# A decay mix with a routed low-rank layer on one Trainium2 core: a partial sum in the third group, the second group's routing one scan later, weight chunks in another order

## What is computed

```python
ek, ekv = exp(min(f, 30)), exp(min(f, 30)) * f
nf, df = scan(a = a*decay + ekv), scan(b = b*decay + ek)       # forward in time
nb, db = the same two, backward in time
euk  = exp(min(u + f, 30))
y    = sigmoid(x) * (nf + nb - ekv + euk*f) / max(df + db - ek + euk, 1e-8) * gain
h      = silu(y @ rw1.T + rb1)                                  # 64 wide
logits = (h @ rw2.T + rb2)[:, :16] + gates
coeff  = softmax over the two largest logits, 0 elsewhere       # 16 experts
base   = y @ W.T + bias                                         # 1024 x 1024
delta  = ((y @ A.T) * coeff) @ B                                # 16 experts of rank 16
out    = x + base + delta
```

## Time and profile before

| | us |
|---|---|
| median of 3 runs | 656.72 |
| lowest and highest | 656.48, 657.44 |
| the profiled execution, its own time | 657.03 |
| its span in the trace (first to last instruction) | 654.9 |
| TensorE busy | 586.5 |
| VectorE busy | 506.1 |
| GpSimd busy | 374.6 |
| ScalarE busy | 372.1 |

### The profile page before, as it was taken

The page is one execution under the profiler, slowest core; times in us unless marked ns, Lnnn a source line. Parts: engine busy times, 40 slices in busy tenths (PEclk is TensorE's granted clock), DMA queues, the critical chain, the costliest instruction groups (busy, mean ns, idle before and its releaser), DMA issues.

```text
span 654.9 us, 6960 instructions
## 1 busy us (share of the span) xinstructions
PE 586.5 (90%) x2562; PEld 472.7 (72%) x2562; DVE 506.1 (77%) x562; ACT 372.1 (57%) x446; POOL 374.6 (57%) x190
## 2 busy tenths in 40 slices
PE   0145899989989979999999989999999999999997
PEld 0134686768867857888788867888788878888786
DVE  7999999999989999998999989997899121032202
ACT  6788899979759775648565775486355310020100
POOL 1799999999949955765566657575357201000100
PEclk9977899999989989999999999999999999999999
DMA  6335566576716821786142722354132303050112
GB/s 201 119 103 181 175 209 181 159 163 130 149 56 126 198 94 38 178 219 208 49 145 72 249 65 78 116 175 146 49 113 87 122 0 97 0 161 1 49 48 81
DMA packets 32097, 78.45 MB, mean 120 GB/s; under 512 B 4608, under 2 KB 4800, under 8 KB 32064
## 3 DMA queue, kind: packets, MB, share of 16 engines
q1 hardware_dynamic: 28608, 69.62, 33.1%
q0 software_dynamic: 3456, 8.39, 7.9%
HBM read 57.03 MB, written 25.17 MB: 126 GB/s over the span
## 4 chain that ended last, share of the span: by engine, by line
PE 47%; DVE 26%; POOL 11%; issue 6%; ACT 6%; DMA 4%; SPq 0%; POOLq 0%; DVEq 0%; ACTq 0%
PE acc L1071 15%; PE acc L1073 14%; PE acc L1072 14%; DVE mix L866 4%; DVE mix L861 4%; DVE mix L857 4%; DVE mix L888 3%; DMA yr<-x_cm 2%; POOL mix L727 2%; POOL y_lo L737 2%; DVE eu L876 2%; DVE yr L895 2%; POOL mix L702 2%; POOL yr L708 2%; DVE kv L871 1%
## 5 line engine op out<-in xcount | busy, mean ns | idle before, releaser
L1071 PE MATMUL acc<-y_hi,wa_hi 128*128 128x512 f32 x638 | 254.9, 400 | 51.0 <-POOL y_lo L737 46.2
L1072 PE MATMUL acc<-y_lo,wa_hi 128*128 128x512 f32 x638 | 251.3, 394 | 0.0
L1073 PE MATMUL acc<-y_hi,wa_lo 128*128 128x512 f32 x638 | 251.2, 394 | 0.0
L1071 PEld LDWEIGHTS acc<-y_hi,wa_hi 128*128 128x128 f32 x638 | 121.8, 191 | 80.8 <-POOL y_lo L737 48.0
L1073 PEld LDWEIGHTS acc<-y_hi,wa_lo 128*128 128x128 f32 x638 | 121.5, 190 | 26.0
L1072 PEld LDWEIGHTS acc<-y_lo,wa_hi 128*128 128x128 f32 x638 | 121.9, 191 | 24.7
L727 POOL TENSOR_TENSOR mix<-mix,kv 128x1024 f32<-128x1024 f32 x30 | 74.8, 2495 | 69.2 <-DVE mix L844 69.2
L737 POOL TENSOR_TENSOR y_lo<-yr,y_hi 128x1024 fp32r<-128x1024 f32 x31 | 76.7, 2475 | 33.8 <-ACT y_hi L441 33.8
L909 DVE SCALAR_TENSOR_TENSOR xo<-acc,bias_sb,xo 128x512 f32<-128x512 f32 x48 | 35.5, 741 | 73.6 <-PE acc L1073 73.5
L750 POOL TENSOR_TENSOR wx_lo<-xa,wx_hi 128x512 fp32r<-128x512 f32 x16 | 21.2, 1404 | 111.6 <-ACT wx_hi L529 111.6
L702 POOL TENSOR_TENSOR mix<-mix,kv 128x1024 f32<-128x1024 f32 x31 | 76.8, 2478 | 3.8 <-DVE mix L888 3.8
(11 more groups left out here) (129 smaller groups left out, 726.2 us busy)
## 6 DMA issues: line engine op xcount, KB each, us to landing
kv<-f_cm SPq DMA_DIRECT2D x32, 512.0 KB, 3.6
yr<-x_cm SPq DMA_DIRECT2D x32, 512.0 KB, 3.6
out<-xo SPq DMA_DIRECT2D x64, 256.0 KB, 3.6
xo<-x_cm SPq DMA_DIRECT2D x48, 256.0 KB, 3.9
out<-x_cm POOLq DMA_DIRECT2D x8, 512.0 KB, 7.8
out<-xo POOLq DMA_DIRECT2D x16, 256.0 KB, 7.1
xa<-w_base SPq DMA_DIRECT2D x5, 512.0 KB, 3.6
xo<-w_base SPq DMA_DIRECT2D x3, 512.0 KB, 4.3
```

What stands on the lines that cost most here:

```text
L1071: nc.tensor.matmul(out_ap, wh, yh, start=start, stop=False)
L1072: nc.tensor.matmul(out_ap, wh, yl, start=False, stop=False)
L1073: return nc.tensor.matmul(out_ap, wl, yh, start=False, stop=stop)
```

## The change

Four things are changed.

1. **The chunks.** The weights' last router chunk (channels of units 6 and 7) moves behind the last two base chunks: its casts move from step 5 to step 7, and the chunks behind it move within their steps.
2. **The `x` additions.** `add_x(4)` moves from the end of step 8 to the start of step 9, `add_x(6)` and `add_x(7)` in step 9 behind `split_wx(0)` and `split_lo(8)`.
3. **The routing of group 1** stands behind the scan `forward_num(12)` and no longer ahead of it.
4. **A partial sum in group 2.** Output block 0 of group 2 is summed over the first six units only (`late_part`) in the bank of j = 0, copied out by ScalarE at step 15 (`drain_late_part`) and stored by SP. The bank then takes block 3, whose first six depths are summed right there (`block_of` swaps blocks 0 and 3 of this group). Block 0 comes back as tile 19 (`LATE`), with the last two depths and the experts' part only; GpSimd adds it to the output by an accumulating DMA at step 19 (`add_late`) in the place of SP's store, and the load of tile 25, that reuses the buffer, waits for that DMA (`late_added`).

```diff
@@ -113,16 +113,16 @@
         chunks = [("base", 0), ("base", 1), ("base", 2), ("base", 3), ("router_a", 0, 3), ("base", 4), ("router_a", 3, 6),
-                  ("base", 5), ("router_a", 6, CB), ("base", 6), ("base", 7), ("expert", 0), ("expert", 1)]
+                  ("base", 5), ("base", 6), ("base", 7), ("router_a", 6, CB), ("expert", 0), ("expert", 1)]
         CHUNKS = len(chunks)
-        router_a_chunk = [4, 4, 4, 6, 6, 6, 8, 8]
-        base_chunk = [0, 1, 2, 3, 5, 7, 9, 10]
-        load_steps = [[], [2, 3], [4], [5], [7], [9], [11], [12]]
-        load_late_steps = [[], [], [], [6], [8], [10]]
-        hi_steps = [[1], [2], [3, 4], [5], [7], [9], [10], [11]]
-        hi_mid_steps = [[], [], [], [], [6], [8], [], [], [12]]
-        lo_steps = [[0], [1], [2], [3], [5], [7], [9], [10], [11], [12]]
-        lo_late_steps = [[], [], [], [4], [6], [8]]
+        router_a_chunk = [4, 4, 4, 6, 6, 6, 10, 10]
+        base_chunk = [0, 1, 2, 3, 5, 7, 8, 9]
+        load_steps = [[], [2, 3], [4], [5], [7], [9], [10], [11]]
+        load_late_steps = [[], [], [], [6], [8], [], [], [12]]
+        hi_steps = [[1], [2], [3, 4], [5], [7], [8], [9], [11], [12]]
+        hi_mid_steps = [[], [], [], [], [6], [], [], [10]]
+        lo_steps = [[0], [1], [2], [3], [5], [7], [8], [9], [], [12]]
+        lo_late_steps = [[], [], [], [4], [6], [], [], [10], [11]]
@@ -162,8 +162,16 @@
+        LATE_DEPTH, LATE_SLOT, LATE = CB - 2, 2, SPLIT * CB + 3
+        LATE_NEXT = next(e for e in range(PARTS, 2 * PARTS) if e % XBUF == LATE_SLOT)
+
+        def block_of(G, j):
+            return (3, 1, 2, 0, 4, 5, 6, 7)[j] if G == SPLIT else j
+
         def base_from(G, j=0):
-            return part_depth[G * CB + j] if G < SPLIT else 0
+            if G < SPLIT:
+                return part_depth[G * CB + j]
+            return LATE_DEPTH if G * CB + j == LATE else 0
@@ -185,7 +193,8 @@
         AFTER_GATE, AFTER_LO = range(2)
-        x_adds_at = {(CB, AFTER_LO): (4, 5), (CB + 1, AFTER_GATE): (5, 6), (CB + 1, AFTER_LO): (6, 8),
+        BEFORE_SUM = 2
+        x_adds_at = {(CB + 1, BEFORE_SUM): (4, 5), (CB + 1, AFTER_GATE): (5, 6), (CB + 1, AFTER_LO): (6, 8),
                      (THIRD + 1, AFTER_LO): (0, 2), (THIRD + 2, AFTER_LO): (2, 4)}
@@ -205,8 +214,8 @@
         silu_at |= {(CB, AFTER_SCALE): 0, (THIRD, AFTER_FWD): SPLIT, (FIFTH, AFTER_BWD_NUM): 4}
-        routing_at = {(first_step(G) + 1, AFTER_FWD): G for G in (1, 5, 6, 7)}
-        routing_at |= {(CB, AFTER_BWD_NUM): 0, (first_step(3) + 1, AFTER_BWD_DEN): 3}
+        routing_at = {(first_step(G) + 1, AFTER_FWD): G for G in (5, 6, 7)}
+        routing_at |= {(CB, AFTER_BWD_NUM): 0, (first_step(1) + 1, AFTER_FWD_NUM): 1, (first_step(3) + 1, AFTER_BWD_DEN): 3}
         routing_at |= {(THIRD, AFTER_FWD_NUM): SPLIT, (FIFTH + 1, AFTER_RATIO): 4}
@@ -230,7 +239,7 @@
         def stores_to(slot, end):
-            return sum(1 for e in range(PARTS, end) if e % XBUF == slot)
+            return sum(1 for e in range(PARTS, end) if e % XBUF == slot and e != LATE)
@@ -245,6 +254,10 @@
         part_out = sem("part_out")
+        late_part_done = sem("late_part_done")
+        late_part_out = sem("late_part_out")
+        late_part_stored = sem("late_part_stored")
+        late_added = sem("late_added")
         x_added = [sem(f"x_added{j}") for j in range(CB)]
@@ -349,11 +362,17 @@
                         sp.wait_ge(out_stored[e % XBUF], 16 * stores_to(e % XBUF, e))
+                if e == LATE_NEXT:
+                    sp.wait_ge(late_part_stored, 16)
+                if e - XBUF == LATE:
+                    sp.wait_ge(late_added, 16)
                 sp.dma_start(xo[:, e % XBUF, :], at(x_cm, e)).then_inc(x_in[e % XBUF], 16)
...
                     load_x(e + AHEAD)
+                if e == LATE:
+                    return
                 sp.wait_ge(evacuated, evacuations(e))
@@ -389,6 +408,9 @@
                     load_x(e)
+                if s == THIRD - 1:
+                    sp.wait_ge(late_part_out, 1)
+                    sp.dma_start(at(out, LATE), xo[:, LATE_SLOT, :]).then_inc(late_part_stored, 16)
                 for p in tiles(parts_at, s - 1, PART_END):
@@ -535,6 +558,11 @@
                 nc.scalar.copy(xo[:, 2 + p % PBUF, :], acc[:, p % 5, :]).then_inc(part_out, 1)
+
+            def drain_late_part():
+                act.wait_ge(late_part_done, 1)
+                act.wait_ge(out_added[LATE_SLOT], 16 * len(range(LATE_SLOT, PARTS, XBUF)))
+                nc.scalar.copy(xo[:, LATE_SLOT, :], acc[:, out_bank(SPLIT, 0), :]).then_inc(late_part_out, 1)
@@ -623,6 +651,8 @@
                     exp_gap(G)
+                if s == THIRD - 1:
+                    drain_late_part()
                 if 0 < s <= UNITS and not late_split:
@@ -761,6 +791,12 @@
                 nc.gpsimd.dma_start(at(out, e), xo[:, e % XBUF, :], accum_op=ALU.add).then_inc(out_added[e % XBUF], 16)
+
+            def add_late():
+                pool.wait_ge(evacuated, evacuations(LATE))
+                pool.wait_ge(late_part_stored, 16)
+                nc.gpsimd.dma_start(at(out, LATE), xo[:, LATE % XBUF, :],
+                                    accum_op=ALU.add).then_inc(late_added, 16)
@@ -775,16 +811,18 @@
                 if s == CB + 1:
+                    for j in tiles(x_adds_at, s, BEFORE_SUM):
+                        add_x(j)
                     sum_n(s - 1)
...
                     gate_n(s - 1)
+                    split_wx(0)
+                    split_lo(s - 1)
                     for j in tiles(x_adds_at, s, AFTER_LO):
                         add_x(j)
-                    split_wx(0)
-                    split_lo(s - 1)
                     p1(s + 1)
@@ -802,6 +840,8 @@
                     add_out(e)
+                if s == THIRD + 3:
+                    add_late()
                 for n in chunks_at(lo_steps, s):
@@ -906,7 +946,7 @@
                 dve.wait_ge(x_in[e % XBUF], 16 * x_loads_to(e))
-                nc.vector.scalar_tensor_tensor(out=xo[:, e % XBUF, :], in0=acc[:, bank, :], scalar=bias_sb[:, j:j + 1],
+                nc.vector.scalar_tensor_tensor(out=xo[:, e % XBUF, :], in0=acc[:, bank, :], scalar=bias_sb[:, block_of(G, j):block_of(G, j) + 1],
                                                in1=xo[:, e % XBUF, :], op0=ALU.add, op1=ALU.add).then_inc(evacuated, 1)
@@ -1117,7 +1157,7 @@
                 yh, yl = y_of(G, kc)
-                c = slice(ER + j * P, ER + (j + 1) * P)
+                c = slice(ER + block_of(G, j) * P, ER + (block_of(G, j) + 1) * P)
                 return three(acc[:, out_bank(G, j), :], wa_hi[:, kc, c], wa_lo[:, kc, c], yh, yl,
@@ -1129,8 +1169,15 @@
+            def late_part(kc):
+                yh, yl = y_of(SPLIT, kc)
+                c = slice(ER, ER + P)
+                last = three(acc[:, out_bank(SPLIT, 0), :], wa_hi[:, kc, c], wa_lo[:, kc, c], yh, yl, kc == 0, kc == LATE_DEPTH - 1)
+                if kc == LATE_DEPTH - 1:
+                    last.then_inc(late_part_done, 1)
+
             def expert(G, j):
-                c = slice(j * P, (j + 1) * P)
+                c = slice(block_of(G, j) * P, (block_of(G, j) + 1) * P)
                 for a in range(2):
@@ -1200,7 +1247,7 @@
             def depths(G, j):
-                return range(base_from(G, j), CB if G < SPLIT else HALF)
+                return range(base_from(G, j), CB if G < SPLIT or G * CB + j == LATE else HALF)
@@ -1241,10 +1288,19 @@
                     for kc in range(sooner, CB - 1):
-                        while made < (kc if kc == CB - 2 else kc - LAG + 1):
-                            for j in range(2):
-                                base(G, j, made)
-                            made += 1
+                        if kc == CB - 2:
+                            for k in range(made, kc):
+                                late_part(k)
+                            for k in range(made, kc):
+                                base(G, 1, k)
+                            pe.wait_ge(late_part_out, 1)
+                            for k in range(kc):
+                                base(G, 0, k)
+                        else:
+                            while made < kc - LAG + 1:
+                                late_part(made)
+                                base(G, 1, made)
+                                made += 1
                         unit_in(G, kc)
@@ -1334,7 +1390,8 @@
                         for j in range(3, CB):
-                            last = base(G, j, kc)
+                            if G * CB + j != LATE:
+                                last = base(G, j, kc)
                         last.then_inc(slot_free, 1)
```

5 lines of the change are left out of this document (3 added, 2 removed).

## The result

The changed kernel takes 659.66 us (median of 6 runs, 658.71 to 660.27) against 656.93 us of the kernel before, run beside it (6 runs, 656.43 to 657.44). The ratio is 1.004 with an interval of 1.0029 to 1.005: 2.7 us slower by the medians. The forecast was 657.8 us, with 655.2 to 660.6 as its range. The profiled execution took 659.57 us (span 657.1), 2.5 us above that of before, 2.2 of them in the span.

The account below looks back on a forecast made before the run. VectorE's scans set the pace until 396 us, then TensorE alone, so an edit counts by moving that last stage's start. Load and cat -0.4, cold start +1.5: +1.1 us on 656.72, median 657.8 us, range 655.2 to 660.6.

Parts of the forecast that it names:

- The front: Moved router chunk and x additions, steps 5 to 9: zero, bounds 0.7 us either way on VectorE.
- The `x` additions: Step 9, behind the low halves: TensorE gains up to 1 us at 142 us, hidden because VectorE sets the pace.
- The routing: Second group: the scan fills VectorE's 2.33 us pause, all that follows is 2.2 us earlier, bounds 0 to 2.3.
- The hidden layer: Third group: of VectorE's 1.32 us wait, 0.2 us gained, bounds 0 and 1.3.
- The lead at step 19: VectorE 2.4 us ahead after 252 us, so unit 18's gate, before the accumulating DMA, ends at 291.2.
- Its landing: The accumulating DMA, ahead of SP's load of tile 25, takes 5.2 us and lands at 296.4, before 296.8.
- The rivals of a quick or a late landing: Accumulating DMA: quick, 3.8 to 4.0 us, -0.3 to -0.1, chance 0.12; late, 7.1 to 8.4, +3.0 to +4.3, chance 0.18.
- The queue behind it: SP's queue after the accumulating DMA: unchanged, 4.89 us to the issue of unit 20's load, 5.25 to land.
- The cold start: TensorE waits 7 us before the fourth group's cat, restarts at the 1.2 GHz level and loses 1.5 us.
- Sum: Load and cat -0.4, cold start +1.5: +1.1 us at 318 us, unchanged to the end.

Follow-up runs that it names:

- old_chunks: The changed kernel with the chunk order and chunk steps of the kernel before, the x additions still moved: 658.48 us, ratio 1.0020.
- old_x_adds: The changed kernel with the additions of x back where they were: 662.38 us, ratio 1.0070.
- old_route: The changed kernel with the second group's routing back ahead of the numerator's forward scan: 660.96 us, ratio 1.0063.
- only_route: The kernel before with the routing move alone: 655.20 us, ratio 0.9976.
- combined: The changed kernel with old chunk order, earlier x loads for units 20 and 24, three depths of the fourth group's block 2 before cat's transposition: 650.65 us.
- early_r: The changed kernel with the load of x for unit 20 moved ahead of the load of tile 25 on SP's queue: 654.28 us, ratio 0.9963.
- warm: The changed kernel with seven depths of the fourth group's block 2 (21 matmuls) made before the transposition of cat: 656.20 us, ratio 0.9987.

## Where the prediction held and where it was off, point by point

The direction and its main mechanism held: a lead of VectorE that the SP queue eats, and a cold start that nothing covers. The chances lay evenly between "within 0.2%" (0.43) and "slower" (0.42); it was slower by 0.4%, and the time came out 1.9 us above the forecast. Step by step:

- **The front, taken as 0 with bounds of 0.7: wrong, +1.13 us** (forward scan at 178.26, before 177.13). This is the term that was sized worst, and it lies outside its own bounds. I counted casts on ScalarE and instructions on GpSimd, and said that what VectorE gains in step 5 it gives back in step 7. It gave back more: +0.44 us by 117 us (two casts stand ahead of the logarithm, wait 0.93 instead of 0.22), then 1.25 us of blocking by the chunk that lands beside a VectorE instruction in step 8 (0.75 us of pause took up a part), then 0.18 at the exponential. I had not listed the low half that moves in step 8 at all. old_chunks gives 1.3 us back. The four executions with these tables and additions scatter by 0.5 us at this point, so 1.13 is one reading of some 0.9.
- **The `x` additions, taken as hidden.** TensorE's wait for `wx_lo` did fall, 1.38 to 0.23, and that is hidden as said. That `add_x(4)` also moves the low half that VectorE collides with was missed; it is worth 2.0 us (old_x_adds), so this move, with the chunks, is no side matter.
- **The routing: right, 1.93 us instead of 2.2.** At the backward scan behind it (186.86, before 187.93, with the front 1.13 late) the gain is the whole 2.20, in spite of the exponential; the rest goes at the product with `xa`, which now waits 0.16 us for TensorE. TensorE's own wait for this product fell from 2.69 to 0.78 us. That the gain depends on what the front does was not in the forecast (old_route).
- **The hidden layer: 0.38 instead of 0.2.** The 18 matmuls fit as said.
- **The lead at step 19 was therefore 1.20 us, not 2.4.** The accumulating DMA went out at 292.29, not 291.2.
- **Its landing: 5.07 us, forecast 5.2.** In the eight other kernels that have it, it took 4.9 to 5.9. The rivals of a quick or a late landing were not needed, and nine more rows, 4.9 us and up, disagree with the estimate of 2.6 us by the Trainium skill (DMA: Bandwidth & Descriptors, Anatomy of one DMA). The queue behind it took 0.33 less than forecast (297.36 to 301.92, 4.56 for 4.89). So the load came +0.26 instead of -0.4: 1.09 - 0.13 - 0.33 + 0.04 = 0.67 us off, nearly all the front.
- **The cold start: 2.0 us, forecast 1.5.** I scaled from seven starts after 2.69 us of idle time; here the transposition and nine starts fall into the slow phase before `spread`.
- **Sum**: 0.26 + 2.0 = +2.2 us of span, 0.67 (load) and 0.5 (cold start) above the forecast of 1.1. Of the profiled execution's 2.5 us the remaining 0.3 lie outside the span. The medians differ by 2.7, and the kernel before had 656.93 beside the changed one, where the forecast started from 656.72.

The parts alone give 3.4 - 1.6 and, for chunks and additions together, 1.3 (old_chunks undone): 3.1, measured 2.6 in common. That this comes out within the intervals of about 1 us is in part luck, since the parts don't simply add up: the front and the routing overlap in the wait for the logits (old_route).

Open is why the executions of most variants spread over some 4 us (old_chunks 657.1 to 661.5, only_route 654.0 to 658.6), those of combined over less than 2 (650.3 to 652.2). The traces hint at two places. One is the load of `x` for unit 24: VectorE's wait behind it is 0 in the changed kernel, 0.96 in early_r, 1.01 in old_route and 1.21 in old_chunks; combined moves this load and the one for unit 20. The other is the clock: at the same place, behind the second group's routing, TensorE idled 2.69 us and restarted at 0.56 in the kernel before, and idled 2.64 us and kept 1.00 in old_route. One profile of each kernel doesn't settle it.

## What to carry to other kernels

Before a wait is added on a queue, list what stands behind it: here one load of `x` that had nothing to do with the waited-for tile stood there, and moving that one command was worth 5.0 us: it turned a loss of 2.6 into a gain of 2.4. A lead of an engine is worth nothing until the next thing it waits for comes earlier too, and a wait as long as the 5.81 us here costs twice, since a cold start of 2.0 us followed it; filling it with matmuls that are due anyway gained 3.5 us (warm). When work is moved on GpSimd, look at what VectorE runs at the new place, not only at the order of the queue. And a delay isn't lost where a later wait can take it up: removing that wait, as the routing move does, lets the delay through.
